# Second attention of a two-layer transformer: row maxima by two 64-row matmuls and one reduction over two banks

## The reference

```python
# x: (1, 2048, 128), 16 heads of 64
qkv = (layernorm(x) * gamma + beta) @ w_qkv   # q, k, v per head: (2048, 64)
q, k = rotate(q), rotate(k)                   # rotary embedding
scores = einsum('bhid,bhjd->bhij', q, k) * 64 ** -0.5
probs = softmax(scores, axis=-1)
out = einsum('bhij,bhjd->bhid', probs, v)
```

## Time and profile before

| | us |
|---|---|
| median of three runs | 3532.42 |
| the three runs | 3528.71 to 3536.83 |
| profiled execution | 3523.92 |
| its span | 3522.1 |
| second attention's maxima and heads, first reduction to last exponential | 2061.0 to 3337.4 |
| busy in the span: TensorE, VectorE, ScalarE, GpSimd | 3026.6, 2903.7, 2990.3, 2561.3 |

### The profile page before, as it was taken

The page is one execution under the profiler, slowest core; times in us unless marked ns, Lnnn a source line. Parts: engine busy times, 40 slices in busy tenths (PEclk is TensorE's granted clock), DMA queues, the critical chain, the costliest instruction groups (busy, mean ns, idle before and its releaser), DMA issues. The chain is left out here.

```text
span 3522.1 us, 61429 instructions
## 1 busy us (share of the span) xinstructions
PE 3026.6 (86%) x19520; PEld 1281.0 (36%) x19520; DVE 2903.7 (82%) x4260; ACT 2990.3 (85%) x2784; POOL 2561.3 (73%) x1562
## 2 busy tenths in 40 slices
PE   6888888888888888888886868888888888888899
PEld 4122121222222222222113415555555555555547
DVE  7989999999999999999998968887877778788421
ACT  3999999999999999999994828887878778788942
POOL 5888888888888888888681517777767777677850
PEclk9788777887778877788777959999999999999999
DMA  2000000000000000000001641000001110000000
GB/s 75 5 8 7 7 6 1 7 7 7 3 4 7 7 7 2 4 7 7 11 1 39 218 110 34 25 26 26 25 26 38 31 32 25 26 25 25 19 22 13
DMA packets 59537, 85.71 MB, mean 24 GB/s; under 512 B 9808, under 2 KB 45904, under 8 KB 58960
## 3 DMA queue, kind: packets, MB, share of 16 engines
q1 hardware_dynamic: 59344, 83.06, 8.2%
HBM read 52.44 MB, written 30.54 MB: 24 GB/s over the span
## 5 line engine op out<-in xcount | busy, mean ns | idle before, releaser
L1238 POOL TENSOR_TENSOR lo<-pr,hi 128x1024 f16<-128x1024 f32 x384 | 917.5, 2413 | 384.1 <-ACT hi L1364 381.9
L1287 DVE TENSOR_REDUCE mx<-mx_ps 128x1 f32<-128x512 f32 x1024 | 660.1, 684 | 165.1 <-PE mx_ps L1402 161.8
L1379 ACT ACTIVATE pr<-s_ps 128x1024 f32<-128x1024 f32 x512 | 531.7, 1038 | 264.1 <-PE s_ps L1423 232.8
L1364 ACT ACTIVATE hi<-pr 128x1024 f16<-128x1024 f32 x512 | 548.0, 1071 | 0.0
L1402 PE MATMUL mx_ps<-ka,qa 128*128 128x512 f16 x1024 | 385.3, 397 | 142.0 <-DVE mx L1287 117.5
L722 ACT ACTIVATE wt<-wt 128x2048 f32<-128x2048 f32 x256 | 485.3, 1896 | 0.5
L713 ACT ACTIVATE wt<-wt,theta_bias 128x2048 f32<-128x2048 f32 (+2 forms) x160 | 482.5, 3015 | 3.4 <-DVE wt L563 2.7
L501 POOL TENSOR_TENSOR wt<-base,wt 128x1024 f32<-128x1024 f32 x192 | 460.2, 2397 | 16.0
L501 POOL TENSOR_TENSOR wt<-vb,wt 128x1024 f32<-128x1024 f32 x192 | 454.8, 2369 | 16.0
L1442 PE MATMUL pv_ps<-vh,hi 128*128 128x129 f16 x4096 | 432.6, 222 | 10.9 <-ACT sums L1370 5.3
L1421 PE MATMUL s_ps<-qa,ka 128*128 128x512 f16 x1024 | 396.1, 387 | 35.4 <-issue 20.9
(11 more groups left out here) (208 smaller groups left out, 5050.1 us busy)
## 6 DMA issues: line engine op xcount, KB each, us to landing
qk<-stg SPq DMA_DIRECT2D x6, 2048.0 KB, 11.1
vh<-v SPq DMA_DIRECT2D x16, 520.0 KB, 3.4
qa<-qk SPq DMA_DIRECT2D x16, 512.0 KB, 3.6
ka<-qk SPq DMA_DIRECT2D x32, 256.0 KB, 4.6
v<-v_st SPq DMA_DIRECT2D x3, 2080.0 KB, 7.9
qst<-parts_dram SPq DMA_DIRECT2D x144, 32.0 KB
kst<-parts_dram SPq DMA_DIRECT2D x144, 32.0 KB
qk<-stg SPq DMA_DIRECT2D x4, 1024.0 KB, 7.8
```

The lines of the kernel that those rows point to most:

```text
L1238: eng.tensor_tensor(lo[:, i % NHL, :, :], pr_slot(i), hi[:, i % NHL, :, :], ALU.subtract).then_inc(lo_done, 1)
L1287: eng.tensor_reduce(mx4[:, q // NCH, q % NCH:q % NCH + 1], mx_ps[:, q % 2, :], AX.X, ALU.max)\
L1364: eng.activation(hi[:, i % NHL, :, :], pr_slot(i), ACT.Copy).then_inc(hi_done, 1)
L1379: eng.activation(pr_slot(i), s_ps[:, i % 2, :, :], ACT.Exp, scale=SM).then_inc(exp_done, 1)
```

## The change

Five things are changed, all in `stage_attention1`.

1. **Pairs.** A maximum is now taken from high part times high part only, over 64 partitions. `mx_pair` issues two matmuls: one on partitions 0 to 63 (`qa`, `ka`) into bank 0 of `mx_ps`, one on partitions 64 to 127 into bank 1. The second needs q's high part in the upper partitions, in a new tile `qc` (in the memory of `xn2`, printed as `two`), and a sixth transfer of 256 KB a head. There are 32 pairs a head. VectorE reduces both banks by one instruction (`reduce_pair`). A pair may be written when the reduction of the previous pair is done.
2. **Slots.** Each step has four places for a pair: before the scores, between their halves, behind them, and in the middle of the weighing. Pairs stand 3.125 slots apart from step 2 on.
3. **Half lows.** VectorE's low is two instructions of 512 elements, the first at its old step and the second one step later. In a step with two pairs the half stands between their reductions.
4. **First maxima in chunks.** Before the first scores stand only 8 pairs, a quarter of head 0. The other 24 and the 32 of head 1 follow within head 0, two or three a step, with a transpose, a copied row and a small transfer for each further quarter.
5. **TensorE's loop over head pairs** is a Python loop: all heads are written out. VectorE's and SP's remain loops.

The core of the diff:

```diff
-    NMX = NT * NCH
+    NMX = NT * NCH // 2
     MX0, MX1 = 2, STEPS - 5
-    mx_at = [min(NMX, max(0, -(-NMX * (i - MX0) // (MX1 - MX0)))) for i in range(STEPS + 1)]
+    SLOTS = 4
+    mx_slot = [SLOTS * MX0 + SLOTS * (MX1 - MX0) * q // NMX for q in range(NMX)]
+    NQ1 = NMX // NS
+    FIRST = [2] * (NS * 4 - 4) + [3] * 2 + [2] * 13
+    TURN0 = [4 * c for c in range(1, NS)]
...
                     for dst, src, sem_ in ((qa[:, par, :], q[h, :, :], loaded),
+                                           (qc[HD1:P, par, :], q[h, 0:HD1, :], loaded),
                                            (ka[0:HD1, par, :], k[h, 0:HD1, :], loaded),
...
-                def reduce_bank(h, q):
-                    eng.wait_ge(mx_done, NMX * h + q + 1)
-                    eng.tensor_reduce(mx4[:, q // NCH, q % NCH:q % NCH + 1], mx_ps[:, q % 2, :], AX.X, ALU.max)\
-                       .then_inc(mx_taken, 1)
+                def reduce_pair(h, q):
+                    eng.wait_ge(mx_done, 2 * NMX * h + 2 * q + 2)
+                    j, c = 2 * q // NCH, 2 * q % NCH
+                    eng.tensor_reduce(mx4[:, j, c:c + 2], mx_ps[:, :, :], AX.X, ALU.max).then_inc(mx_taken, 1)
...
+                def low_half(h, i, n_):
+                    if n_ == 0:
+                        eng.wait_ge(hi_done, STEPS * h + i + 1)
+                        eng.wait_ge(pv_done, STEPS * (h + 2) + i + 1 - NHL)
+                    ins = eng.tensor_tensor(lo[:, i % NHL, n_, :], pr[:, i % NPR, n_, :], hi[:, i % NHL, n_, :],
+                                            ALU.subtract)
+                    if n_ == 1:
+                        ins.then_inc(lo_vector, 1)
...
+                        for hq, q in pairs[:cut]:
+                            reduce_pair(hq, q)
+                        for n_ in range(2):
+                            at = i - LOW - n_
+                            if (at >= 0 or not first) and on_vector(at):
+                                low_half(h, at, n_)
+                        for hq, q in pairs[cut:]:
+                            reduce_pair(hq, q)
...
-                def mx_bank(h, par, q):
+                def mx_pair(h, par, q):
                     if q == 0:
-                        eng.wait_ge(loaded, 16 * 3 * (h + 1))
+                        eng.wait_ge(loaded, 16 * 4 * (h + 1))
...
                     eng.wait_ge(mx_taken, NMX * h + q + 1)
-                    j, c = q // NCH, q % NCH
-                    eng.matmul(mx_ps[:, q % 2, :], qa[:, par, j * P:(j + 1) * P],
-                               ka[:, par, c * BANK:(c + 1) * BANK], start=True, stop=True).then_inc(mx_done, 1)
+                    j, c = 2 * q // NCH, 2 * q % NCH
+                    for b, (src, rows) in enumerate(((qa, slice(0, HD1)), (qc, slice(HD1, P)))):
+                        eng.matmul(mx_ps[:, b, :], src[rows, par, j * P:(j + 1) * P],
+                                   ka[rows, par, (c + b) * BANK:(c + b + 1) * BANK], start=True, stop=True)\
+                           .then_inc(mx_done, 1)
...
-                for q in range(NMX):
-                    mx_bank(0, 0, q)
-                mx_turn(0)
+                for q in range(NQ1):
+                    mx_pair(0, 0, q)
+                first_turn(0)
                 scores(0, 0, 0)
                 one(0, 0, first=True)
                 one(0, 1)
-                with eng.Fori(1, H // 2 - 1) as g:
+                for g in range(1, H // 2 - 1):
```

More of the change, by code:

```diff
@@ L1318, in one @@
                     for i in range(STEPS):
+                        if first:
+                            pairs = [divmod(q, NMX) for q in range(first_at[i], first_at[i + 1])]
+                        else:
+                            pairs = [(h + 1, q) for q in pairs_in(i)] if not last else []
+                        cut = len(pairs) // 2 if first else 1
+                        if first and i in TURN0:
+                            first_row(i // 4)
+                        for hq, q in pairs[:cut]:
[6 more added lines that the diff above has]
+                            reduce_pair(hq, q)
+                        if first and i + 1 in TURN0:
+                            first_maxima((i + 1) // 4)
                         if not last:
-                            for q in range(mx_at[i], mx_at[i + 1]):
-                                reduce_bank(h + 1, q)
                             if i == MX1:
@@ L1327, in one @@
                             take(h - 1 if i == SUM else h, (i // KP - 1) % NS)
-                        if (i >= LOW or not first) and on_vector(i - LOW):
-                            low(eng, h, i - LOW, lo_vector)
                     if last:
-                        for i in range(STEPS - LOW, STEPS):
-                            if on_vector(i):
-                                low(eng, h, i, lo_vector)
+                        for n_ in range(2):
+                            low_half(h, STEPS - 1, n_)
                         take(h, NS - 1)
-                for q in range(NMX):
-                    reduce_bank(0, q)
-                maxima(0)
-                row(0)
+                for q in range(NQ1):
+                    reduce_pair(0, q)
+                first_maxima(0)
+                first_row(0)
                 one(0, 0, first=True)
@@ L1416, in scores @@
+                def scores(h, par, i, between=()):
+                    if isinstance(h, int) and h == 0:
+                        if i % KP == 0:
+                            eng.wait_ge(mrow_loaded, 16 * (i // KP + 2))
+                    elif i == 0:
+                        eng.wait_ge(mrow_loaded, 16 * (h + NS + 1))
                     eng.wait_ge(exp_done, STEPS * h + i + 1)
@@ L1437, in weigh @@
                     for n_ in range(2):
+                        for at in between if n_ == 1 else ():
+                            mx_pair(*at)
                         k = 2 * kp + n_
@@ L1462, in one @@
                         if i >= SUM or not first:
-                            weigh(h, par if i >= SUM else 1 - par, i - SUM)
+                            weigh(h, par if i >= SUM else 1 - par, i - SUM, () if first else after)
+                        for at in after if first else ():
+                            mx_pair(*at)
                     if last:
```

87 lines of the change are left out of this document (67 added, 20 removed).

## The result

| | before | forecast | after |
|---|---|---|---|
| median of the runs, us | 3533.23 | 3550 | 3682.00 |
| lowest and highest | 3528.71, 3536.83 | range 3480 to 3612 | 3673.19, 3690.05 |
| profiled execution, us | 3523.92 | 3542 | 3686.69 |
| second return of the small reduction of a head | 2177.18 | about 2195 | 2201.15 |
| mean head after that (14 heads) | 78.0 | 77.5 | 88.0 |

The ratio is 1.042, with an interval of 1.039 to 1.045. The sign was forecast; the size was not, and the time lies above the range. The whole miss is in the heads: 14 x (88.0 - 77.5) = 147 us, and 3542 + 147 = 3689, where the profiled execution took 3686.7.

A forecast was written before the change was run, and what follows sets the result against it. No single engine bounds the maxima stretch; the engines wait in turn. Loop -35, fourteen heads +31 and start +22 sum to +18 us: 3542 for the profiled execution, 3550 against the median, range 3480 to 3612.

The forecast's parts named there:

- Term 1: TensorE's loop over head pairs: writing it out removes five "issue" waits of some 4 us, -35 us.
- Term 3: Start and head 0: first scores 28 us earlier, but more pairs lie in head 0; +22 us, bounds +14 and +33.
- Reduction, pair and gap: Maxima stretch: two-bank reduction 1.21 us, then a gap of 0.56 us, 16 gaps open a head; uncovered pair 1.77 us.
- Case D: Maxima pairs don't stand together or are hemmed in by drains: gap of 0.70 us, total 3592 us, chance 0.14.
- case B: Short handoff between maxima pairs: gap of 0.48, halves of 1.0 us, load no later; total 3484 us, chance 0.28.
- Load at the head: Start of the maxima stretch: first pair waits for the sixth transfer; first reduction at 14.1 instead of 12.2 us, +1.9 a head.
- The failed step: VectorE's half low in the maxima stretch: takes 1.12 us, bounds 1.0 and 1.2.
- The same step for the divisions: VectorE's divisions in the maxima stretch: 0.97 us each, 3 of them in steps 2 to 26.
- case C: Maxima stretch: a tenth of the 25 steps falls to the low clock level, +67, total 3617 us, chance 0.13.

## Why the prediction was wrong in size

- **Term 1, the loop: right.** -35 forecast, -40 measured (33 to 52); no "issue" wait is left.
- **Term 3, the start: right.** The second small reduction moved by 24 us (forecast 22, which gives 2199; the prediction also says "near 2195"; it came at 2201.15). The first scores started at 2084.1 and not 2080.4, since the first reduction itself came 3.9 us later than forecast.
- **Reduction, pair and gap: right.** 1.219 us, starts 0.01 apart, 0.52 us for a short gap (0.56 forecast), and about 16 gaps a head. Case D did not occur, and the gap lies halfway to case B, which it couldn't bring about.
- **Load at the head: right.** The prediction named "over 2 us" for the first pair's wait. TensorE waits 29.2 us for ka in 14 heads, 2.1 a head (3.23 in the head shown above), and the rest is 13.7 where 14.1 was forecast.
- **The failed step: "half a low is (2.09 + 0.15) / 2 = 1.12 us (bounds 1.0 and 1.2)".** It took the mean duration as work and split it by elements, and had no term for a wait behind GpSimd. Of the 2.05, 1.20 is work and 0.85 a wait. If each half pays that again it takes 0.67 + 0.85 = 1.52; measured are 1437 ns over all and 1.65 in the stretch. That is 6.8 us a head, 95 in 14, far outside the bounds.
- **The same step for the divisions.** They also read SBUF alone; 4.9 us a head instead of 2.9, 28 in 14. In the kernel before, the last of the three operations never took over 0.43 us; the second took 1.9 in one place of a head, but outside the stretch. That divisions meet GpSimd's instructions more often now is what the timelines show; why just here follows from no experiment.
- **Late gaps and the clock (case C, in part).** The stretch ran at 0.91, under the 0.98 that the prediction named for C. The late gaps are 5.5 a head of over 0.6 us. The one of 1.36 us before 2495.02 shows how one arises (TensorE, timeline):

```profile
2490.84 0.60 PE L1468 MATMUL mx_ps<-ka,qa 64*128 64x512 f16 x1
...
2492.58 0.29 PE L1525 MATMUL pv_ps<-vh,hi 128*128 128x129 f16 x1 [0.16 <-DVE lo L1360]
...
2493.88 0.53 PE L1498 MATMUL s_ps<-qa,ka 128*128 128x512 f16 x1
...
2494.56 0.39 PE L1468 MATMUL mx_ps<-ka,qa 64*128 64x512 f16 x1
```

  TensorE had stood 1.47 us before the pair at 2489.10 and went over to its low level by 2490.84: a pair's matmul takes 0.60 us there and 0.39 at the level of 2.4 GHz. The weighing, held for the half low of 2490.70 by only 0.16 us, then took 1.30 us (2492.58 to 2493.88) instead of 0.69, so the next pair was late for VectorE. The forecast put the clock apart from the lows, as a rival of its own with a chance of 0.13. With short GpSimd instructions and the same matmuls the clock is 0.99, so here it is mostly a consequence; the run without VectorE lows, at 0.91, shows that the halves are not the only wait that can bring it down. Gaps came to 11.5 us instead of 9.6, 27 us in 14 heads.

95 + 28 + 27 = 150 us, against the 147 that were missing. This is a sum of rows of one run; the three were not measured apart. The forecast was right in direction partly by luck: it had the heads 2.2 us longer for the load and the gaps, and they were 10.5 us longer again, mostly for a wait that it did not have.

## What to carry to other kernels

Where VectorE and GpSimd both work from SBUF, read the shortest duration of an instruction beside its mean: the shortest is the work, the difference is a wait that comes with each instruction. Cutting VectorE's instruction in two made it 1.4 to 2 times as long here (0.85 us a low to 1.17, 0.82 to 1.54, 0.44 to 0.92). To shorten it, cut GpSimd's instruction, and look afterwards at the longest duration on VectorE, not at the mean alone: halves brought 0.8% here on the old order, and quarters lost it again, mostly in eight instructions. And count an instruction's price in a serial handoff by its wait, since TensorE's waits, and with them its clock, follow.

## What the hardware showed that was not expected

- A VectorE subtraction of 512 elements took 0.67 us beside an idle GpSimd and up to 2.66 beside one running 1024-element instructions. Two back to back took up to 5.04.
- A VectorE addition that needs 0.39 us took 7.61 beside a row of 256-element GpSimd instructions without a gap: shorter instructions on GpSimd don't bound the wait.
- A GpSimd subtraction takes 2.11 us for 1024 elements, 1.15 for 512 and 0.66 for 256, so about 0.18 us of start-up.
- The wait goes both ways: GpSimd's own low took 2413 ns on average in the kernel before, 2256 after, and 2112 at the shortest.
- Of the 190 us that parts 1 to 4 cost, no single change on VectorE's or TensorE's side won back more than about 20. A change on GpSimd, the engine with the lowest busy share of the four (68%), won back all.
